# A three-block Trainium2 kernel (gated FFN, gated slot attention, FFN): where one batch's rows are prepared, and where small sums and filling matmuls stand

## The reference

```
x = x + 0.5 * ffn(layernorm(x))          # "block one" below
x = x + attn(layernorm(x))               # 16 heads of 128
x = x + 0.5 * ffn(layernorm(x))

ffn(x):  q(w) = clip(round(w / (mean|w| + 1e-8)), -1, 1)
         (sigmoid(x @ q(w1).T) * (x @ q(w2).T)) @ q(w3).T
attn(h): q, k, v, w = silu(conv4(h @ W)); w = l2norm(w); beta = sigmoid(h @ Wb)
         g = log_sigmoid(h @ Wf1 @ Wf2)
         step t: Sk = Sk*exp(g) + k (beta*w);  Sv = Sv*exp(g) + (beta*w) v
                 a = softmax(q @ Sk * scale);  o = a @ Sv
         o = rmsnorm(o) * norm_w * sigmoid(h @ Wg1 @ Wg2 + bg2);  o @ Wo
```

## Time and profile before

| | us |
|---|---|
| median of 3 runs (2808.47 to 2810.02) | 2809.45 |
| the profiled execution, its own time | 2808.98 |
| its span, first to last instruction | 2807.1 |
| PE busy in it | 2757.3 (98%) |
| DVE, ACT, POOL busy | 2229.9, 1671.3, 1425.0 |
| mean granted TensorE clock, share of full speed | 0.997 |

### The profile page before, as it was taken

One profiled execution on the slowest core, in us unless ns is written; L12 is line 12 of the kernel. 1 busy time (PEld: TensorE's weight loads), 2 busy tenths in 40 slices (PEclk: granted clock), 3 DMA queues, 4 the chain that ended last, 5 costly groups with the idle time before them and its releaser, 6 DMA issues. The chain is left out here.

```text
span 2807.1 us, 43427 instructions
## 1 busy us (share of the span) xinstructions
PE 2757.3 (98%) x13814; PEld 1933.3 (69%) x13814; DVE 2229.9 (79%) x5777; ACT 1671.3 (60%) x3777; POOL 1425.0 (51%) x2122
## 2 busy tenths in 40 slices
PE   7999999999999999999999999999999999999999
PEld 5887566666666666666666666666666666666887
DVE  7554588988888899888888888888889888884543
ACT  5111677677777677776777677677677777760110
POOL 0200466666566666665666666656666666660000
PEclk9999999999999999999999999999999999999999
DMA  4500211111112111111121111111212111105000
GB/s 169 195 16 28 66 36 35 35 50 35 50 35 69 52 57 35 50 35 49 35 72 50 57 35 51 33 50 35 72 51 60 35 50 38 51 24 199 15 16 30
DMA packets 90932, 151.06 MB, mean 54 GB/s; under 512 B 9297, under 2 KB 30929, under 8 KB 90193
## 3 DMA queue, kind: packets, MB, share of 16 engines
q1 hardware_dynamic: 90704, 148.29, 16.8%
HBM read 127.02 MB, written 21.23 MB: 53 GB/s over the span
## 5 line engine op out<-in xcount | busy, mean ns | idle before, releaser
L1552 PE MATMUL ps<-hT,space 128*128 128x512 f32 x2048 | 996.1, 594 | 1.1 <-ACT hT L1023 1.1
L902 POOL TENSOR_TENSOR s<-s,tmp 128x256 f32<-128x256 f32 (+1 forms) x448 | 367.2, 820 | 302.7 <-DVE tmp L1219 281.4
L1552 PEld LDWEIGHTS ps<-hT,space 128*128 128x128 f32 x2048 | 345.9, 191 | 194.8 <-issue 167.6
L902 POOL TENSOR_TENSOR X<-S,D 128x256 f32<-128x256 f32 x384 | 275.9, 718 | 108.6 <-ACT S L1077 82.5
L1596 PEld LDWEIGHTS ps<-Y,S 128*128 128x128 f32 x1536 | 220.8, 191 | 151.3 <-issue 133.7
L333 ACT ACTIVATE sig<-up_ps 128x512 f32<-128x512 f32 x88 | 52.7, 599 | 406.7 <-PE up_ps L542 406.5
L542 PE MATMUL up_ps<-h_hi,wq 128*128 128x512 f32 x704 | 281.1, 399 | 2.2 <-DVE h_lo L404 2.1
L1584 PEld LDWEIGHTS ps<-AM,XT 128*128 128x128 f32 x1536 | 216.5, 191 | 94.6 <-issue 90.1
L902 POOL TENSOR_TENSOR Y<-aT,D 128x256 f32<-128x256 f32 x384 | 280.5, 752 | 0.0
L542 PE MATMUL up_ps<-h_lo,wq 128*128 128x512 f32 x704 | 278.3, 395 | 0.0
L902 POOL TENSOR_TENSOR A<-ident,dg 128x512 f32<-128x512 f32 x64 | 66.6, 1041 | 390.0 <-DVE space L1296 384.2
(11 more groups left out here) (187 smaller groups left out, 6383.2 us busy)
## 6 DMA issues: line engine op xcount, KB each, us to landing
space<-in_wk_dram SPq DMA_DIRECT2D x64, 256.0 KB, 2.6
space<-in_ww_dram SPq DMA_DIRECT2D x64, 256.0 KB, 2.6
space<-in_wq_dram SPq DMA_DIRECT2D x64, 256.0 KB, 2.7
space<-in_wv_dram SPq DMA_DIRECT2D x64, 256.0 KB, 2.7
space<-in_wo_dram SPq DMA_DIRECT2D x64, 256.0 KB, 3.2
wq_dram<-wq SPq DMA_DIRECT2D x3, 2816.0 KB, 19.4
space<-in_w_dram SPq DMA_DIRECT2D x8, 704.0 KB, 10.9
x_sb<-in_x_dram SPq DMA_DIRECT2D x4, 1024.0 KB, 5.4
```

Source lines behind the costliest of these rows:

```text
L902: return nc.gpsimd.tensor_tensor(out, in0, in1, op)
L1552: mm = nc.tensor.matmul(bank[x][:, :], ck_(slot[x], kk), hT[n // NH % 2][:, kk, :], start=(kk == 0), stop=(kk == KT - 1))
```

## The change

It does six things.

1. Quantisation sums: `total(1)` stands behind the first gate half tile instead of before it; `total(2)` behind up tile 2 instead of behind the two first tiles; `threshold(2)` and `quantise(2, 0)` behind `hidden(0, 1)` instead of behind `hidden(0, 0)`.
2. The 16 transposes of batch 0's rows for the attention block stand in block one, in its last batch after tiles 7 and 8, and ACT's new `copy_rows` copies them to hT and hR there. Those two tiles take the place of `res`, `sq`, `osq` in the memory that outlives the block.
3. Block one's DVE also norms batch 1: `norm_stats(NB + 1)` after tile 9, `norm_apply(NB + 1)` after tile 10, before `add_output(NB - 1)`.
4. The load, `row_stats`, `deviation` and `norm_rows` of batch 1 in the attention block are gone, and its eight steps stand in turns 1 to 8 instead of 8 to 15. Batches 2 and 3 stay.
5. In the last turn `last_rows(0)` stands before `sT`, `last_rows(1)` behind it, `(2)` and `(3)` before `onT`. The last unit's `onT` uses bank 5, `last_rows(1)` bank 7.
6. ACT and DVE wait once, in turn 0, for the stores of block one, since `sq` now lies where its tiles lay.

```diff
@@ ffn_phase
-                if b + 1 < NB and m >= MT - 4 and m < MT - 2:
+                if (b + 1 < NB or first) and m >= MT - 4 and m < MT - 2:
                     turns.append(("rows", b + 1, m - (MT - 4)))
...
+            def copy_rows(half):
+
+                for k in (2 * half, 2 * half + 1):
+                    source = up_ps[k % 2][pair["rows", NB, half]]
+                    act.wait_ge(ln_transposed, KT * NB + k + 1)
+                    nc.scalar.activation(standing["hT"][:, k, :], source[:, :], ACT.Copy).then_inc(rows_copied, 1)
+                    nc.scalar.activation(two_blocks(standing["hR"][:, k, :]), odd_in(source),
+                                         ACT.Copy).then_inc(rows_copied, 1)
...
-                    if first and b == 0 and m == 0:
+                    if first and b == 0 and m == 1:
                         threshold(2)
                         quantise(2, 0)
-                    if first and b == 0 and m == 1:
                         quantise(2, 1)
                         quantise(2, 2)
...
+                    if first and b == NB - 1 and m == MT - 2:
+                        norm_stats(NB + 1)
+                    if first and b == NB - 1 and m == MT - 1:
+                        norm_apply(NB + 1)
...
             if first:
                 total(0)
-                total(1)
                 pair_free(("tile", 0, 0))
                 up_half(0, 0, 0)
+                total(1)
                 pair_free(("tile", 0, 1))
                 up_half(0, 1, 0)
                 up_half(0, 0, 1)
                 up_half(0, 1, 1)
-                total(2)
...
                         up_tile(b, m)
                         if first and b == 0 and m == 2:
+                            total(2)
                             down_tile(0, 0)
@@ attention_phase
+        def outputs_bank(u):
+
+            return psum[5] if u == UNITS - 1 else bank["onT"]
...
+        def step_in(n):
+
+            return n - 1 if n < NH else n % NH - ROWS_FROM
+
         def prepared_in(n):
 
-            return n // NH + 1 if 0 <= n < UNITS - NH and n % NH >= ROWS_FROM else None
+            return n // NH + 1 if 0 <= n < UNITS - NH and 0 <= step_in(n) < len(PREPARED) else None
...
-                if early and 0 <= n % NH - STATS_FROM < C:
+                if early and n >= NH and 0 <= n % NH - STATS_FROM < C:
                     row_stats(n // NH + 1, n % NH - STATS_FROM)
...
-                if n == 0:
-                    for kk in range(KT):
-                        transpose_rows(0, kk)
-                    pe.wait_ge(act_edge, after(ACT_EDGE, "hT3", 0))
...
+                if n == UNITS:
+                    pe.wait_ge(wo_last_full, 16 * C)
+                    pe.wait_ge(dve_late, after(DVE_LATE, "m64", u))
+                    last_rows(0, 0, 1, 2)
                 if late:
                     pe.wait_ge(pool_late, after(POOL_LATE, "ad64", u))
                     transpose("sT", lambda c: ck_(s, c), pe_late)
                 if n == UNITS:
-                    pe.wait_ge(wo_last_full, 16 * C)
-                    pe.wait_ge(dve_late, after(DVE_LATE, "og", UNITS - 2))
-                    last_rows(0, 0, 1, 2)
+                    last_rows(1, 0, 1, 2)
...
                 if n == UNITS:
-                    last_rows(1, 0, 1, 2)
+                    last_rows(2, 0, 1, 2)
+                    last_rows(3, 0, 1, 2)
...
                     transpose("onT", lambda c: on[:, c, :], pe_late)
-                if n == UNITS:
-                    last_rows(2, 0, 1, 2)
-                    last_rows(3, 0, 1, 2)
```

More of the change, by code:

```diff
@@ L45 @@
 Q_EPS = 1e-8
+HALF = T // 2
 def standing_tiles(nc, ctx, a):
@@ L64, in standing_tiles @@
     t["wo"] = [take(HID) for _ in range(C)]
-    t["res"], t["sq"], t["osq"], t["unused"] = take(C, HID), take(C, P), take(C, P), take(C, P)
+    t["hT"], t["hR"], t["unused"] = take(KT, T), take(KT, HALF), take(C, P)
     t["mask"] = {l: take(T // 2) for l in LEVELS}
@@ L168, in ffn_phase @@
         by_compare = [(0, 0), (0, 1), (1, 0), (1, 1), (0, 2), (1, 2), (2, 0), (2, 1)]
-        normed = [b + 1 for b in range(NB)] if not first else [b for b in range(NB + 1)]
+        normed = [b + 1 for b in range(NB)] if not first else [b for b in range(NB + 2)]
         if not first:
@@ L369, in _ @@
                         sigmoid(b, m)
+                    if first and b == NB - 1 and m >= MT - 4 and m < MT - 2:
+                        copy_rows(m - (MT - 4))
         @block.vector
@@ L516, in pair_free @@
                     what, b, at = user
-                    if what == "rows":
+                    if what == "rows" and b == NB:
+                        pe.wait_ge(rows_copied, KT * (at + 1))
+                    elif what == "rows":
                         pe.wait_ge(h_split, 2 * KT * b + KT * (at + 1))
@@ L617 @@
 UNITS = NB * NH
-HALF = T // 2
 def pat(t, at, *dims):
@@ L737, in attention_phase @@
         hold = sb("hold", [P, 1])
-        res, sq, osq, unused = (standing[n] for n in "res sq osq unused".split())
+        res, sq, osq, unused = sb("res", [P, C, HID]), sb("sq", [P, C, P]), sb("osq", [P, C, P]), standing["unused"]
         stats = sb("stats_a", [P, C, 6])
@@ L744, in attention_phase @@
         rstd = sb("rstd_a", [P, C])
-        hT = [sb(f"hT{i}", [P, KT, T]) for i in range(2)]
-        hR = [sb(f"hR{i}", [P, KT, HALF]) for i in range(2)]
+        hT = [standing["hT"], sb("hT1", [P, KT, T])]
+        hR = [standing["hR"], sb("hR1", [P, KT, HALF])]
         f1T = [sb(f"f1T{i}", [P, T]) for i in range(2)]
@@ L873, in _ @@
                 load_slot("gate", u)
-                if u % NH == 1:
+                if u % NH == 1 and u > NH:
                     sp.wait_ge(pe_edge, after(PE_EDGE, "lnT3", u // NH))
@@ L943, in turn @@
                     add_level(64, pool_late)
-                if early and n % NH == STATS_FROM + C - 1:
+                if early and n >= NH and n % NH == STATS_FROM + C - 1:
                     deviation(n // NH + 1)
@@ L1306, in gated_even @@
                     nc.vector.scalar_tensor_tensor(even_chunks(og[:, u % (2 * C), :]),
-                                                   two_blocks(bank["onT"][:, 0:HALF]), norm_w[:, 0:1],
+                                                   two_blocks(outputs_bank(u)[:, 0:HALF]), norm_w[:, 0:1],
                                                    even_chunks(sg), ALU.mult, ALU.mult).then_inc(dve_late, 1)
@@ L1311, in gated_odd @@
                     nc.vector.scalar_tensor_tensor(odd_chunks(og[:, u % (2 * C), :]),
-                                                   odd_blocks_reversed(bank["onT"]), norm_w[:, 0:1],
+                                                   odd_blocks_reversed(outputs_bank(u)), norm_w[:, 0:1],
                                                    odd_chunks(sg), ALU.mult, ALU.mult).then_inc(dve_late, 1)
@@ L1328, in turn @@
                     level_scores(64, dve_late)
-                if early and 0 <= n % NH - STATS_FROM < C:
+                if early and n >= NH and 0 <= n % NH - STATS_FROM < C:
                     row_stats(n // NH + 1, n % NH - STATS_FROM)
-                if early and n % NH == NORM_FROM:
+                if early and n >= NH and n % NH == NORM_FROM:
                     norm_rows(n // NH + 1, 0)
                     norm_rows(n // NH + 1, 1)
-                if early and n % NH == NORM_FROM + 1:
+                if early and n >= NH and n % NH == NORM_FROM + 1:
                     norm_rows(n // NH + 1, 2)
@@ L1385, in turn @@
                 if early:
+                    if n == 0:
+                        dve.wait_ge(loaded, 16 * (NB - 1 + C))
                     dve.wait_ge(act_early, after(ACT_EARLY, "sq", n))
@@ L1484, in _ @@
                 pe.sem_inc(done, len(steps))
+            pe.sem_inc(pe_edge, KT)
             def transpose_rows(b, kk):
-                if b > 0:
-                    pe.wait_ge(dve_edge, after(DVE_EDGE, "xn3", b))
+                pe.wait_ge(dve_edge, after(DVE_EDGE, "xn3", b))
                 for c in range(C):
@@ L1563, in transpose @@
                 def transpose(name, src, done, count=C):
+                    into = outputs_bank(u) if name == "onT" else bank[name]
                     for c in range(count):
-                        last = nc.tensor.transpose(ck_(bank[name], c), src(c), ident[:, :])
+                        last = nc.tensor.transpose(ck_(into, c), src(c), ident[:, :])
                     last.then_inc(done, 1)
@@ L1665, in turn @@
                     if coming is not None:
-                        pe.wait_ge(act_edge, after(ACT_EDGE, PREPARED[n % NH - ROWS_FROM], coming))
+                        pe.wait_ge(act_edge, after(ACT_EDGE, PREPARED[step_in(n)], coming))
                     project("q", 0)
```

20 lines of the change are left out of this document (12 added, 8 removed).

## The result

The changed kernel takes 2813.81 us (median of 20 runs, 2808.91 to 2815.75), the kernel before 2808.59 in 20 runs beside it: ratio 1.0019, 95% interval 1.0012 to 1.0025. That is 5.2 us slower; I had said 2809.7, at most 2812.8. The profiled execution took 2815.18 us, 1.4 above its median (that of the kernel before took 2808.98, 0.4 above), its span is 2813.4 against 2807.1, its mean granted clock 0.994 against 0.997. So what follows explains 6.3 us of one execution, a little more than the 5.2 of the medians.

A forecast was written before the change was run, and what follows sets the result against it. TensorE, busy 98% of the span, was taken as the bound, with about 50 us of waits to win. Terms +2.3 - 0.9 + 0 + 0 - 1.1 = +0.3 us on the median 2809.45 gave 2809.7, range 2806.3 to 2812.8.

The forecast's parts named there:

- I take the same loss: zero in the sum: Block change: the low clock would cost the projections the same 2.3 us as before, so 0 in the sum.
- Everywhere else PE's rows follow without a gap: Outside four places touched by the change, work moved between dense turns was to cost there what it saves here.
- The start, +2.3.: Start of block one: moved sums make the first down tile start at 39.65 against 37.33; bounds -1.1 to +2.6.
- the new places of the sums pay: Rival at the start: only the early start counts, -1.1 instead of +2.3, total 2806.3 us; chance 0.06.
- The slower rival: the clock falls at the start: Rival: two gaps before the first down tile drop the clock, +3.4 us, total 2813.1; chance 0.07.
- Neither 1.60 nor 2.75 alone did it: Argument against the slower rival: single PE gaps of 1.60 and 2.75 us had not dropped the clock before.
- The block change, -0.9.: Block one to attention: PE goes on at 283.4 where the projection began at 284.26; bounds -2.3 to +1.0.
- The rival that it would stay up: Block change: the clock stays up through the 3.4 us gap, -2.3 us, total 2807.4; chance 0.15.
- The aside that the place would give 2.1 without the norm in between: Block change: without batch 1's norm ahead of the add, the gain would be 2.1 us instead of 0.9.
- Batch 1's preparation, 0.: Turns 1 to 8: moved steps win nothing, as transposes push u_v and its gap stays; bounds -1.7 to +0.4.
- The last turn, -1.1.: Last turn: sT 0.4 late, 2.6 us of filler gone from the end, new wait of 1.1; bounds -1.5 to +0.4.
- clock and sums: Two rivals together, clock up at the block change and sums paying: 2804.0 us, the edge of faster by over 0.2%.

The follow-up runs named there:

- e13: Changed kernel with spare matmuls at the start (18, 6, 8), at the block change (11) and one in each of turn 0's three gaps; 2807.14 us.
- e8: Kernel before with 18 spare matmuls behind total(0) and 7 behind block one's last down tile; 2807.35 us.
- e9: Kernel before with only total(1) moved behind the first gate half tile; 2807.69 us.
- e10: Kernel before with only total(2) and its threshold moved; 2809.82 us.
- e6: Changed kernel with the old sums, batch 1's statistics and norm one tile earlier, and last_rows(3) behind the transposes of on; 2805.47 us.
- e1: Changed kernel with total(1), total(2), threshold(2) and quantise(2, 0) back in their old places; 2808.28 us.
- e15: Changed kernel unaltered, 11 more runs and a second profile; 2813.32 us.
- e4: Changed kernel with last_rows in the old places of the last turn, new banks kept; 2813.43 us.
- e5: Kernel before with parts 2, 3, 4 and 6 alone, plus the new banks of part 5; 2810.68 us.
- e2: Kernel before with only the quantisation sums moved; 2811.39 us.
- e7: e6 with 18 spare matmuls behind total(0) and 7 behind block one's last down tile; 2802.2 us.

## Why the prediction was wrong

**The step that failed** is the sentence "I take the same loss: zero in the sum" for the clock, and that the clock was asked about at two places alone. It measured +5.5 us in the profile, at five places. With the low clocks taken away, those that the kernel before had as well, the changed kernel is 6.2 to 6.7 us faster (e13). Behind it stands another sentence, "Everywhere else PE's rows follow without a gap": turn 0 and the start of the third block have gaps, and the clock fell there.

- *The start, +2.3.* Right, and by its working: 39.50 against 39.65, and 2.4 in e13 against e8, where the clock plays no part. That `total(1)` alone costs next to nothing was right as well (e9, 0.2); but `total(2)` alone costs 1.0 (e10), and the rest comes only with both. The rival "the new places of the sums pay" is out.
- *The slower rival: the clock falls at the start.* It happened, at 41 us after gaps of 1.45 and 2.09, where I had given it 0.07. "Neither 1.60 nor 2.75 alone did it" was true and no argument: there were two gaps (and 2.75 alone is no safe size either: in e10 the clock falls right behind a wait of 2.74 us for s, at 2515). A clock under 1.00 between 37 and 46 was among the signs that I had named for being wrong. It cost 1.6, not 3.4. Its total of 2813.1 is near the result by chance: the rest came from places that it doesn't name.
- *The block change, -0.9.* It was -0.7: PE started 1.58 us behind the add and not 1.29. The clock cost 0.8 more than before, inside the bounds of -2.3 and +1.0. The rival that it would stay up is out: behind the gap of 3.61 it was low for 6.8 us. The aside that the place would give 2.1 without the norm in between was too high: e6 has the norm elsewhere, and its gap is 0.9 us shorter than e1's, not 1.2. By the rule of the Trainium skill, "TensorE: Matmul & The Clock Gate", Part 4 on PE-mode transposes, that they don't count as busy, the new gap was the shorter one; no gain came of it. e9 and e10 have the old gap, transposes in its middle, and no low clock behind it (ten records in 4.56 us), where the kernel before lost 6.8 us of it. Neither the rule nor its contrary can be read from that.
- *Batch 1's preparation, 0.* Right. The waits for `u_v` stayed at 1.3, nothing was swallowed, and the four transposes of turns 1 to 4 came back in turns 8 to 15. But turn 0 lost 1.5 us by the clock, where I had looked at no clock at all. Before, PE waits there three times within 7 us (1.00, 1.13 and 0.94), and none of the three was in my rows.
- *The last turn, -1.1.* -0.9 by the order of the work (the new wait is 0.97 for my 1.1, `last_rows(0)` came 0.5 late for my 0.4), and +0.5 by the clock.
- *The range.* Two of its cases were added up only downwards ("clock and sums"). Upwards I asked for a "longer low clock at the block change" and gave 0.03. Here, with PE busy 98% of the time, gaps that were made, moved or only came later lost the clock, and nearly all of these losses went in one direction.

**Shown:** the order of the work costs about 1 us (0.8 in the account, 1.2 between the profiles of e13 and e8), where I had said 0.3, and the clock makes the rest, 4 to 5.5 us (e13 beside e15; the busy time at the same count of matmuls). **Open:** why the clock falls in the last turn and at the start of the third block. The same gaps of 0.61, 1.25, 0.69 and 0.83 us bring it in the changed kernel and don't in e13, and with the old places it falls in e4, e5, e9 and e10 and not in e2, e8 nor in the kernel before. What differs at the same gaps is what ran before them and when they come, and no run here varies that alone. No run filled gaps there.

## What to carry to other kernels

Where TensorE is the bound, compare its busy time at the same count of instructions before looking for waits: here more busy time with no more work was the clock, and no list of waits showed it. It is an upper figure, since a wait can take up what stands ahead of it. Price a new gap on PE twice, once for its length and once for what the matmuls behind it lose, up to the next wait that another engine sets, and go through every cluster of gaps in the program, also those that the change doesn't touch. And before giving up a reordering that lost, try useless matmuls in its gaps, sized by a row of the same type: here they turned 5.2 us lost into none, and the 0.11% that the best order won (e6) into 0.19% (e7).

## What I had not expected of the hardware

- The stretches at half clock in the column came in two lengths, 3.4 and 6.8 us, in all profiles of this case (the end of the program aside).
- The column can miss a stretch at the start of the program. In e5 it reads 1.00 from 22 to 28 us, but a matmul is 0.43 us from start to start there, twice the 0.23 of later ones:

```profile
22.00:28.00 6.00, 5.96 (x15) 1.00 0.84 309
```

```profile
26.90 0.63 PE L563 MATMUL up_ps<-h_hi,wq 128*128 128x512 f32 x1
27.32 0.63 PE L563 MATMUL up_ps<-h_lo,wq 128*128 128x512 f32 x1
```

  So a run's mean clock can be too good, and the rows themselves decide.
- A place at which nothing was changed can gain or lose its low clock from one kernel to the next: at the same gap of 3.6 us, ten records of projection took 7.54 us in the changed kernel, 7.16 in its repetition and 5.94 in e1; the last turn of e13 kept the clock with the gaps with which the changed kernel lost it.
- Added matmuls made the kernel faster: e13 has 32 + 11 + 3 more than the changed kernel and is over 6 us shorter.
- Runs of one kernel differ by their clock: in the changed kernel 2808.91 us goes with 0.999 and 2815.25 with 0.994.
